# Summing one batch of mixture-of-experts outputs on TensorE inside the expert stage

## The reference, cut to what matters

```python
E, K, CAP, I = 64, 8, 64, 96
logits = x @ gate_w.T                      # x: the 1024 normalised tokens
probs = softmax(logits)
w, sel = top_k(probs, K)                   # 8 experts a token
w = w / sum(w)
pos = position of the token in its expert's queue
valid = pos < CAP                          # 64 slots an expert
inp[eid, slot] = x[tok]
h = silu(inp @ wg) * (inp @ wu)
out = h @ wd                               # [E, 64, H]
y[tok] += out[eid, slot] * (w * valid)     # 8 terms a token
x = x + tanh(g_ffn[0]) * y
```

## Time and profile before

| | us |
|---|---|
| median of 3 runs (lowest, highest) | 694.07 (693.53, 694.95) |
| profiled execution, its time | 691.71 |
| profiled execution, span first to last instruction | 690.0 |
| busy in it: PE, DVE, ACT, POOL | 476.0, 505.3, 355.6, 285.8 |

### The profile page before, as it was taken

One profiled execution on the slowest core, in us unless ns is written; L12 is line 12 of the kernel. 1 busy time (PEld: TensorE's weight loads), 2 busy tenths in 40 slices (PEclk: granted clock), 3 DMA queues, 4 the chain that ended last, 5 costly groups with the idle time before them and its releaser, 6 DMA issues.

```text
span 690.0 us, 10497 instructions
## 1 busy us (share of the span) xinstructions
PE 476.0 (69%) x3011; PEld 347.7 (50%) x3016; DVE 505.3 (73%) x1265; ACT 355.6 (52%) x784; POOL 285.8 (41%) x277
## 2 busy tenths in 40 slices
PE   5835777767792677772069999999999998244222
PEld 3311222223482444442068999989989997022012
DVE  4277999999865055587548978877887886887854
ACT  2575555554282222223046676666566666575583
POOL 3016777795002633207548448528723331101100
PEclk9955999999896699995579999999999999556555
DMA  6808200000040499922332003203300000000000
GB/s 177 212 0 311 63 0 0 0 31 1 0 153 24 142 343 325 296 93 77 91 107 77 18 13 73 41 1 61 61 0 2 1 1 2 0 16 0 15 15 15
DMA packets 43505, 49.30 MB, mean 71 GB/s; under 512 B 4828, under 2 KB 39238, under 8 KB 43206
## 3 DMA queue, kind: packets, MB, share of 16 engines
q1 hardware_dynamic: 38854, 36.19, 17.2%
q0 software_dynamic: 4608, 12.59, 7.1%
HBM read 42.48 MB, written 6.29 MB: 71 GB/s over the span
## 4 chain that ended last, share of the span: by engine, by line
issue 37%; DVE 19%; POOL 15%; PE 14%; DMA 7%; ACT 4%; another core or an unknown queue 1%; DVEq 1%; POOLq 1%; SPq 1%; ACTq 0%
POOL G L545 7%; DVE hst L1405 7%; DMA wdn<-in_L_ffn_wd 5%; POOL pn L561 4%; PE ps L910 2%; PE ps L1125 2%; DVE hc L1414 1%; DVE ebuf L1528 1%; DVE ebuf L1527 1%; PE ps L1145 1%; POOL dbu L465 1%; PE ps L1023 1%; DVE G L1624 1%; PE ps L934 1%
## 5 line engine op out<-in xcount | busy, mean ns | idle before, releaser
L561 POOL TENSOR_TENSOR pn<-pr,pinv 128x512 f32<-128x512 f32 x64 | 66.9, 1045 | 93.0 <-DVE pinv L1707 92.4
L961 PE MATMUL ps<-hc,ident 128*128 128x512 f32 x128 | 75.0, 677 | 28.7 <-DVE hc L1414 27.3
L465 POOL TENSOR_TENSOR dbu<-du,brow 128x512 f32<-128x512 f32 x64 | 80.6, 1270 | 24.8 <-DVE hst L1405 18.5
L1405 DVE TENSOR_TENSOR_SCAN hst<-ps,dbu 128x512 f32<-128x512 f32 x64 | 77.5, 1212 | 4.3 <-ACT ps L655 4.3
L545 POOL DMA_INDIRECT G<-expert_out,idx_b x64 | 70.3, 1098 | 16.6 <-issue 16.6
L655 ACT ACTIVATE ps<-dtv,amat 128x510 f32<-128x510 f32 x64 | 44.1, 690 | 51.5 <-DVE hst L1405 51.4
L797 ACT ACTIVATE pr<-ebuf,smin 128x256 f32<-128x256 f32 x128 | 63.6, 500 | 8.8 <-DVE smin L1698 8.5
L522 POOL DMA_INDIRECT G<-token_rows,idx_x x32 | 32.3, 1009 | 62.1 <-DVE idx_x L1531 30.7
L961 PEld LDWEIGHTS ps<-hc,ident 128*128 128x128 f32 x128 | 21.0, 202 | 69.5 <-DVE hc L1414 66.7
L1663 DVE TENSOR_TENSOR pT<-ps,pT 128x512 fp32r<-128x512 f32 x64 | 43.9, 686 | 14.0 <-ACT pT L805 12.9
L1698 DVE CUSTOM_DVE_ANT_0 ebuf<-ps,mb 128x256 f32<-128x256 f32 x128 | 48.9, 420 | 1.6 <-issue 1.3
(11 more groups left out here) (288 smaller groups left out, 1496.9 us busy)
## 6 DMA issues: line engine op xcount, KB each, us to landing
wgu<-in_L_ffn_wg SPq DMA_DIRECT2D x15, 384.0 KB
wgu<-in_L_ffn_wu SPq DMA_DIRECT2D x15, 384.0 KB
wdn<-in_L_ffn_wd SPq DMA_DIRECT2D x15, 384.0 KB
expert_out<-xn SPq DMA_DIRECT2D x16, 256.0 KB
wq<-in_L_xattn_Wq SPq DMA_DIRECT2D x1, 2048.0 KB, 9.1
wo<-in_L_xattn_Wo SPq DMA_DIRECT2D x1, 2048.0 KB, 14.6
wo<-in_L_ffn_w SPq DMA_DIRECT2D x2, 1024.0 KB, 7.1
x<-in_x SPq DMA_DIRECT2D x1, 1024.0 KB, 6.7
```

The costliest lines, as they stand in the source:

```text
L465: nc.gpsimd.tensor_tensor(dbu[:, j, :], du[:, j % 2, 512 * hb:512 * hb + 512], brow[:, j // 2, :], ALU.mult).then_inc(pool_dbu, 1)
L561: nc.gpsimd.tensor_tensor(pn[:, h % 2], pr[:, h % 2], pinv[:, h % 2, :].unsqueeze(2).to_broadcast([P, 2, L]), ALU.mult)\
L961: pe.matmul(bank(2 + j % 2), ident[:], hc[:, j % 2, :], start=(isinstance(m, int) and m + k == 0), stop=(isinstance(m, int) and m + k == N ...
L1405: V.tensor_tensor_scan(hst[:, j, :], bank(j % 2), dbu[:, j, :], 0.0, ALU.mult, ALU.add)\
```

## The change

Batch 0 is no longer gathered from DRAM. In the expert stage DVE builds for each slot tile a 0/1 matrix `place` of 128 slots by 256 tokens (slot's token number equal to the column), scales the expert output of each slot by the token's share while copying it out of PSUM, and PE multiplies `place` with it and accumulates all 32 tiles in PSUM bank 7 (`combine`). Each slot's share comes with its token row: `token_rows` grows from H to `ROW = H + E` columns, the last 64 holding the token's shares for all experts. `expert_out` thus holds scaled rows, and for batches 1 to 3 the eight gathered rows are added without weights, by four wide additions a tile instead of eight weighted ones. Slot numbers are worked out for six token tiles instead of eight. The absolute sums of the FFN weights, the rounding and two of the `folded_low` move ahead of the first group on DVE, the rest into groups 3 to 5, 9 and 10; the turning of the rounded weights moves into PE's loop end. `take_rows` waits for `hg_ready` (gated) instead of `xeT_in_psum`. `turn_h` uses one PSUM bank instead of two.

```diff
-        xrows = nc.dram_tensor("token_rows", (B * L + 1, H), F32, kind="Internal").ap()
+        xrows = nc.dram_tensor("token_rows", (B * L + 1, ROW), F32, kind="Internal").ap()
...
             for hb in range(2):
                 sp_.wait_ge(xn_ready, 4 * hb + 4)
-                dma(xrows[512 * hb:512 * hb + 512].rearrange("(c p) h -> p c h", p=P),
+                dma(xrows[512 * hb:512 * hb + 512, 0:H].rearrange("(c p) h -> p c h", p=P),
                     xn[:, 4 * hb:4 * hb + 4, :]).then_inc(d_rows, 16)
+                sp_.wait_ge(chosen_ready, 2 * hb + 2)
+                dma(xrows[512 * hb:512 * hb + 512, H:].rearrange("(c p) e -> p c e", p=P),
+                    share[:, 4 * hb:4 * hb + 4, :]).then_inc(d_rows, 16)
...
             def take_rows(g):
                 if g >= RING:
-                    pool.wait_ge(xeT_in_psum, g - RING + 1)
+                    pool.wait_ge(hg_ready, g - RING + 1)
...
-            for cc in range(2):
-                for k in range(K):
-                    gather(0, cc, k)
             root3(0)
+            for k in range(2):
+                pool.wait_ge(d_eo[k], 16 * (NG // 2))
             attend(0, True, False)
...
             def turn_h(g):
                 pe.wait_ge(hg_ready, g + 1)
-                wait_count(pe, hT_ready, g - 1)
+                wait_count(pe, hT_ready, g)
...
+            def combine(g):
+
+                pe.wait_ge(eo_ready, g + 1)
+                for q in range(2):
+                    for tt in range(2):
+                        last = pe.matmul(ps[:, 7, H * tt:H * tt + H], place[:, g % 2, q, P * tt:P * tt + P],
+                                         eo[:, g % 2, q, :], start=(g + q + tt == 0),
+                                         stop=(g == NG - 1 and q + tt == 2))
+                last.then_inc(summed, 1)
...
+            pe.wait_ge(wabs_ready, 1)
+            pe.matmul(ps[:, 7, 0:2], ones[:], wabs[:], start=True, stop=True).then_inc(summed, 1)
             pe.wait_ge(idx_x_ready, 1)
             turn_rows(0)
-            for g in range(NG + 2):
+            for g in range(NG + 3):
                 if g + 1 < NG:
                     turn_rows(g + 1)
                 if g < NG:
                     gate_up(g)
                 if 1 <= g < NG + 1:
                     turn_h(g - 1)
-                if g > 1:
+                if g > NG:
+                    turn_ternary(g - NG - 1)
+                if 1 < g < NG + 2:
                     down(g - 2)
+                if g > 2:
+                    combine(g - 3)
+            for k in range(2, 4):
+                turn_ternary(k)
...
                 if isinstance(b, int) and b == 0:
-                    pe.wait_ge(eo_ready, NG)
+                    pe.wait_ge(wternT_ready, 4)
...
+            def shares(hb):
+
+                half = slice(4 * hb, 4 * hb + 4)
+                chain.link(V.tensor_reduce(wtop[:], top8[:, half, :], AX.X, ALU.add))
+                chain.link(V.reciprocal(wtop[:], wtop[:]))
+                V.tensor_tensor(share[:, half, :], pexp[:, half, :], wtop[:].unsqueeze(2).to_broadcast([P, 4, E]),
+                                ALU.mult).then_inc(chosen_ready, 1)
...
+            def slot_shares(g):
+
+                dve.wait_ge(d_xe[g % RING], 32 * (g // RING + 1))
+                for e in range(2):
+                    rows = slice(CAP * e, CAP * e + CAP)
+                    for q in range(2):
+                        at = H + GROUP * g + 2 * q + e
+                        chain.step(V.tensor_copy(slot_share[rows, g % RING, q:q + 1], xe[rows, g % RING, q, at:at + 1]))
+
+            def placed(g):
+
+                wait_count(dve, summed, g)
+                for q in range(2):
+                    col = 2 * g + q
+                    chain.step(V.tensor_scalar(place[:, g % 2, q, :], iota_tok, slot_tok[:, col:col + 1], None,
+                                               ALU.is_equal))
+
             def take_out(g):
                 dve.wait_ge(down_done, g + 1)
                 wait_count(dve, d_eo[g % 2], 16 * (g // 2))
-                V.tensor_copy(eo[:, g % 2].rearrange("p q h -> p (q h)"), bank(4 + g % 2)).then_inc(eo_ready, 1)
-
-            gated(0)
-            gated(1)
+                chain.wait()
+                for q in range(2):
+                    last = V.tensor_scalar(eo[:, g % 2, q, :], ps[:, 4 + g % 2, H * q:H * q + H],
+                                           slot_share[:, g % RING, q:q + 1], None, ALU.mult)
+                last.then_inc(eo_ready, 1)
+
+            weight_sums()
+            folded_low(0)
+            folded_low(1)
+            weight_scales()
+            for k in range(3):
+                ternary(0, k)
+            dve.wait_ge(d_rows, 64)
+            dve.wait_ge(consts_ready, 7)
+            for g in range(2):
+                slot_shares(g)
+                gated(g)
             for g in range(NG):
                 if g + 2 < NG:
+                    slot_shares(g + 2)
                     gated(g + 2)
                 if g == 0:
                     choice_ids()
                 if g == 1:
                     choice_slots()
-                if 2 <= g < 2 + NT:
-                    slots_of(g - 2)
-                if g == 2 + NT:
-                    choice_weights()
-                if 10 < g < 15:
-                    folded_low(g - 11)
+                if 2 <= g < NT:
+                    slots_of(g)
+                if g == NT:
+                    choice_indices()
+                if 2 < g < 6:
+                    ternary(1, g - 3)
+                if 8 < g < 11:
+                    folded_low(g - 7)
+                placed(g)
                 take_out(g)
...
+            def add_choices(b, cc, k):
+
+                at = 8 * (b - 1) + 4 * cc
+                wide, into, plus = ((2, 0, 4), (2, 2, 6), (2, 0, 2), (1, 0, 1))[k]
+                for half in range(2):
+                    if k < 2:
+                        dve.wait_ge(d_gath[cc][half], 8 * K * b)
+                if k > 1:
+                    dve.wait_ge(comb_steps, at + k)
+                V.tensor_tensor(G[:, cc, into:into + wide, :], G[:, cc, into:into + wide, :],
+                                G[:, cc, plus:plus + wide, :], ALU.add).then_inc(comb_steps, 1)
...
-                    if 4 <= h < 12 and not last:
+                    if 6 <= h < 8 and not last:
                         for k in range(2):
-                            add_choice(b + 1, h // 4 - 1, 2 * (h % 4) + k)
+                            add_choices(b + 1, 0, 2 * (h - 6) + k)
+                    if 9 <= h < 11 and not last:
+                        for k in range(2):
+                            add_choices(b + 1, 1, 2 * (h - 9) + k)
```

More of the change, by code:

```diff
@@ L1531, in _ @@
             V.tensor_scalar(idx_x[:], ps[:, 0, 0:E // 2], -1.0, float(B * L), ALU.mult, ALU.add).then_inc(idx_x_ready, 1)
+            chain.step(V.tensor_scalar(slot_tok, ps[:, 0, 0:E // 2], -1.0, float(B * L), ALU.mult, ALU.add))
             def choice_ids():
[L1535 removed]
+                for c in range(2, NT):
                     last = V.max_index(eid[:, c, :], top8[:, c, :], pexp[:, c, :])
                 chain.link(last)
[L1538 removed]
+                chain.step(V.tensor_copy(eidf[:, 2:], eid[:, 2:]))
             def choice_slots():
@@ new lines, in ternary @@
+            def ternary(k, step):
+                flat = (w1.rearrange("p a h -> p (a h)"), w2.rearrange("p a b -> p (a b)"))[k]
+                chain.wait()
+                if step == 0:
+                    chain.step(V.tensor_scalar(flat, flat, wscale[:, k:k + 1], MAGIC, ALU.mult, ALU.add))
+                if step == 1:
+                    chain.step(V.tensor_scalar(flat, flat, MAGIC, 1.0, ALU.subtract, ALU.min))
+                if step == 2:
+                    V.tensor_scalar(wtern[k], flat, -1.0, None, ALU.max).then_inc(wtern_ready, 1)
```

143 lines of the change are left out of this document (63 added, 80 removed).

## The result

The changed kernel took 675.51 us (median of 4 runs, 674.87 to 678.02) against 694.51 (693.53 to 695.43, 4 runs): ratio 0.973, 95% interval 0.970 to 0.976. Run again later beside the kernel before on one chip it was 677.36 against 689.48: ratio 0.981, 0.978 to 0.985. So the gain lies between 1.5% and 3%, and the two comparisons do not agree within their intervals. The forecast was 674.5 with a range of 666 to 684. The profiled execution took 675.54 us, with a span of 673.8.

The account below looks back on a forecast made before the run. It saw eight expert groups bound by weight arrival, then 35.2 us with PE nearly idle awaiting batch 0's gathers and sums. Terms +1.7 - 20.4 + 0.8 - 1.5 = -19.4 us gave 674.5 us, range 666 to 684.

Parts of the forecast that it names:

- End of the stage, -20.4: From gate_up(12) to turn_xn3: 33.4 us instead of 53.8, with batch 0's gathers and weighted sums removed.
- The loaded groups, +1.7 (+0.4 to +6): Eight expert groups waiting for weights: wider rows make the period 5.41 us, above PE's 5.25; +1.7 us in all.
- two bounds too close: Rival, chance 0.22: PE at 5.25 and loads at 5.41 lose 0.5 to 0.6 us in each of twelve groups; 681 us.
- The load of the next wdn slot is issued no later: Expert groups: combine stands behind down(g-2), so it does not delay the next wdn load and fills PE's 1.70 us wait.
- the 5.6 us against 5.4: DVE's work in the worst iterations, 3 to 5, against the group period; priced at zero, range zero to +0.6.
- Early work on DVE, zero, hidden by the 7.96 us pause: Before the first gated(): 13.3 us of moved DVE passes make it about 1 us late; without the pause, 1 to 2 us.
- the pause goes: Rival, chance 0.15: the unexplained 7.96 us from 231.46 vanishes and loads start about 6 us earlier; 668.5 us.
- The gathers' issue: POOL in the expert stage: ternary(0) lengthens three early gathers by up to 1.5 us, each placement mask by 0.3; no cost.
- Routing, +0.8: Routing before the expert stage: added shares(0) stands on the path, shares(1) costs +0.1; +0.8 us, bounds 0.2 and 1.7.
- Gathers moved, hidden: Expert stage: take_rows waits for gated, over a period later; at most 18.3 us against four periods, 21.6, so hidden.
- Clock, -1.5: Start of attention: PE idle only about 2 us before turn_xn3, so 2.4 GHz expected; -1.5 us (0 to -2.5).
- Attention, 0 (-2 to +2): Attention heads: POOL or PE is the bound, so halving DVE's additions gains nothing; zero, between -2 and +2 us.

Follow-up runs that it names:

- `wdn` first: Changed kernel with SP issuing the down-weight load ahead of the gate and up loads of two groups later; 674.45 us, ratio 0.978.
- the changed kernel's second trace: The changed kernel profiled once more, unchanged; 677.36 us, gate_up(4) to gate_up(12) 51.41 us.
- late preparation: Changed kernel with the FFN weights' rounding and first folded_low moved from the stage's start into later groups on DVE; 671.09 us, ratio 0.966.
- late preparation and `wdn` first: Changed kernel with DVE's early rounding and folded_low moved into later groups and SP's down-weight load issued first; 668.29 us, ratio 0.969.
- second trace of the kernel before: The kernel before profiled once more, unchanged; 689.88 us, no pause, gate_up(4) 24.43 us after the first gather.
- six-place ring: Changed kernel with DVE's early passes moved later, down-weight loads first, and six places instead of four for gathered token rows; 668.70 us, ratio 0.969.
- narrow additions: Changed kernel with gathered rows added as before, eight 256-column steps a tile, two a head in heads 4 to 11; 679.83 us, ratio 0.978.

## Why the prediction came out as it did

The total came out right, but in part by luck: the stage lost 7.5 us more than the sum had, attention and clock gave back 1.9, and the scatter of the kernel before covered the rest.

*End of the stage, -20.4.* Right: -21.1. 32.85 us measured against 33.4, with combine at 1.83 us for 1.75 and the period without loads 5.21 us for 5.25. Reading PE's price from fold_out and the other steps by the gaps in the earlier trace rows held to 0.2 us each. Only turn_ternary was off, 0.5 us for 0.95, since its row had been taken at the low clock; the prediction had named that as its possible error.

*The loaded groups, +1.7 (+0.4 to +6).* The term that was mis-sized: from the first gather to gate_up(12) the change cost 9.25 us. I had added the rows' bytes to a period at 317 GB/s. What decides is not the rate but the time from the issue of a `wdn` load to its landing. It can be issued 2.9 us after a gate_up starts at the earliest, when down is done, and it is wanted two periods after that start, so with 7.5 us to land the period is (2.9 + 7.5) / 2 = 5.2 us, as it was. With `wdn` first the load takes 8.6 us in the median, which gives 5.75 (measured 46.29 / 8 = 5.79); the 10.0 of the changed kernel's second trace gives 6.45 (measured 51.41 / 8 = 6.43). PE's 5.21 us and the loads' 5.2 stood so close that each late landing became a wait. That is the rival "two bounds too close", only that the loss was 0 to 3.2 us in single groups rather than 0.5 in each, and in the first trace 3.2 of the 9.2 lay in the clock. The 9.25 us lie above the term's own upper bound of +6.

"The load of the next wdn slot is issued no later" was mostly right: 2.9 us after gate_up in seven of nine cases of the second trace, and later than that by 0.6 to 1.3 us in four of nine of the first (the 1.3 is PE's low clock, not SP). In the case below, 3.9 us behind the gate_up of 275.96, SP stood in front of `put`, for which DVE was late. Timeline of DVE and of SP in the kernel after:

```profile
275.50 1.23 DVE L1619 TENSOR_SCALAR wo<-wo 128x2048 bf16<-128x2048 f32 x1
...
277.38 0.88 DVE L1658 TENSOR_SCALAR xn<-ps,wkv 128x256 f32<-128x256 f32 x2
```

```profile
278.29 0.37 SPq L412 DMA_DIRECT2D expert_out<-xn  x1
278.70 0.47 SPq L369 DMA_DIRECT2D wgu<-in_L_ffn_wg  x1
...
279.88 0.51 SPq L378 DMA_DIRECT2D wdn<-in_L_ffn_wd  x1
```

In groups 3 to 5 DVE works without a break, as the 5.6 us against 5.4 had said, and `put` and both loads queue behind its `take_out`. I had priced this at zero because DVE has slack elsewhere; but a queue stood behind it. The load issued 1.0 us late landed in 7.60 and gate_up waited 1.07 for it. With late preparation and `wdn` first the same DVE work stands in these groups and nothing waits, so this is a small part of the loss.

*Early work on DVE, zero, hidden by the 7.96 us pause.* The step was wrong in its reason. The pause was of one execution: it is missing in the second trace of the kernel before and in both after. Against that second trace gate_up(4) comes 5 us later after the first gather (29.3 to 29.8 for 24.4). Taking the early passes away alone brought 0.4 to 0.9 us of it, with `wdn` first 2.8 to 3.3, with two more row places 6.6 to 7.1. The rival "the pause goes" brought no gain either: the loads behind it take back what starts earlier, in the kernel before (1.3 us left of 6.1) as in the six-place ring (0.6 of 3.8).

*The gathers' issue.* Timelines of POOL and of DVE in the kernel after:

```profile
223.02 1.00 POOL L531 DMA_INDIRECT G<-token_rows,idx_x  x1 [0.30 <-issue]
224.33 2.33 POOL L531 DMA_INDIRECT G<-token_rows,idx_x  x1 [0.30 <-issue]
226.96 1.90 POOL L531 DMA_INDIRECT G<-token_rows,idx_x  x1 [0.30 <-issue]
...
253.00 1.43 POOL L531 DMA_INDIRECT G<-token_rows,idx_x  x1 [4.45 <-DVE ebuf L1634]
```

```profile
221.31 2.28 DVE L1601 TENSOR_REDUCE wabs<-wo 128x1 f32<-128x2048 f32 x1
223.50 4.49 DVE L1628 TENSOR_TENSOR mqk<-mqk_full,mqk 128x2048 fp32r<-128x2048 f32 x2
...
228.37 1.52 DVE L1615 TENSOR_SCALAR wo<-wo,wscale 128x2048 f32<-128x2048 f32 x1
...
252.86 0.69 DVE L1585 TENSOR_TENSOR wkv<-wkv 128x512 f32<-128x512 f32 x1
```

Four early gathers took 1.71 to 2.33 us, under the wide subtraction as well as under the rounding passes, but not under the reductions. Later ones took 1.43 when they started beside a slot-number pass with two inputs (L1585), and 1.67 to 1.74 beside a rounding pass. The placement masks, for which I had 0.3 each, lengthened none: the gather at 241.87 took 1.00 us with a mask over its last half. The cost on the path was nil, as the sum had it: with all of them at 1.00 gate_up(4) came less than 1 us earlier. The rule of the Trainium skill ("SBUF — State Buffer", "SBUF: two separate sides") is borne out in kind, but not the 0.3 us that I drew from it for every mask.

*Routing, +0.8.* +0.5 to +1.0 at the first gather. *Gathers moved, hidden.* Right: no late rows in the changed kernel beyond the start, and an earlier release gained nothing.

*Clock, -1.5.* Wrong: PE stood idle for 3.20 us, not 2, and then worked at 0.50 from 336.0 to 340.5, as the kernel before did; the first turning of probabilities came 12.13 us after turn_xn3 against 12.03 there. The step that failed is the clock after the idle stretch, not its price: kept busy, PE stayed at 1.00 and 1.9 us were gained. The term was zero for the kernel as it was changed.

*Attention, 0 (-2 to +2).* -3.4 in the mean of the traces. The narrow additions bring 2.3 to 3.9 of it back (343.88 us, against a mean of 344.24 for the kernel before), so their width and place is the main of it; the run changes both together. I had taken PE's 4.00 of 4.00 in the earlier trace rows as proof that DVE was no bound there; but DVE stood at 3.79 in that row, and in heads 10 and 11 of batch 0 PE had gaps.

So +7.5 in the stage and -1.9 in attention and clock together make the sum about 5 us too good against the mean of the traces; the 2.4 us between the profiled run and the first median, and a kernel before whose time lay between 686.9 and 699.9 over the 31 runs on record, cover it. In the later comparison the gain was 12.1 us, not the 19.4 of the sum: that the first medians differed by 19.0 was luck.

Open: why `wdn` lands later in the changed kernel at all. Row width accounts for 2 to 4 of the 9 us and the order of SP's loads removes 7 in its one trace, but these overlap. The low clock is a rival for part of it: it stood in some groups of one of the changed kernel's two traces and of both of the kernel before, and how much of the 9 it makes is not known. Why late preparation helps in groups 4 to 11 rather than before them was not found.

## What to carry to other kernels

Price a ring's load by issue-to-landing against the periods that it has, not by the mean rate: when another engine's work fills the last idle time beside it, every late landing shows. In a queue of loads put the one with the least time to spare first; here this and the moving of DVE work out of the start gave 7 to 9 us for a few changed lines (8.7 with six row places, beside the changed kernel on one chip). And a pause that nothing in a trace explains is not cover for new work until a second trace shows it too.

## What the runs showed of the hardware

Waits for loads were followed by the lower clock in some cases and not in others. With combine cut to 8 columns PE was busy 10.00 of 10.00 us at 0.50 (1.2 GHz) behind a wait of 3.84 us. In the kernel after, a wait of 1.91 us was followed by a group at 0.59, 3.2 us longer than its neighbours, while the second trace had waits of up to 2.54 us and stayed at 1.00 (2.4 GHz).

A gather's issue on POOL took 1.00 us by itself and beside a 2048-wide reduction on DVE, 1.43 beside a 512-wide pass with two inputs and up to 2.33 beside a 2048-wide one.

A DMA share of 1.0 and more stood beside anything from 283 (1.06) to 317 GB/s (1.04).
